# Spreading a softmax's inverse sums over 64 rows by transfers through device memory instead of by TensorE, ScalarE and VectorE

## What is computed

```python
h = relu(layernorm(x))
q2, k2, v2 = heads(h, ...)                    # two projections each; (16, 384, 64)
scores = einsum('hnd,hmd->hnm', q2, k2) / 8 + mask     # mask from 6144 edges
attn = softmax(scores, axis=-1)
out = einsum('hnm,hmd->hnd', attn, v2)
x = x + out.reshape(384, 1024) @ wo.T + bo
# second layer: relational graph convolution; for each of 8 edge types r:
#   mean_r = (counts_r @ h) / max(count, 1);  u += mean_r @ weight[r]
# third: two SAGE layers; fourth: x @ W.T with a sparse W
```

## Time and profile before

| | us |
|---|---|
| runs of the kernel before | 989.72, 989.1 and one outlier of 1886.29; median 989.72 |
| the profiled execution, device time | 988.7 |
| its span in the trace | 986.9 |
| PE busy in the span | 934.6 (95%) |
| DVE, ACT, POOL busy | 614.1, 368.8, 461.9 |

### The profile page before, as it was taken

One profiled execution on the slowest core, in us unless ns is written; L12 is line 12 of the kernel. 1 busy time (PEld: TensorE's weight loads), 2 busy tenths in 40 slices (PEclk: granted clock), 3 DMA queues, 4 the chain that ended last, 5 costly groups with the idle time before them and its releaser, 6 DMA issues.

```text
span 986.9 us, 13646 instructions
## 1 busy us (share of the span) xinstructions
PE 934.6 (95%) x4743; PEld 823.6 (83%) x4743; DVE 614.1 (62%) x1001; ACT 368.8 (37%) x583; POOL 461.9 (47%) x413
## 2 busy tenths in 40 slices
PE   4999999998999789999999999999999959999994
PEld 4999999997889778888888888888888848878883
DVE  6998888867883525655656556565657366445535
ACT  6333333346883343222222322232243234244311
POOL 5324435455564450756547475474759003216212
PEclk8999999999999989999999999999999979999997
DMA  8998766542345364443453544543333603232301
GB/s 204 243 262 232 207 161 160 144 105 17 50 72 170 65 193 145 115 142 107 143 160 106 162 106 141 150 120 97 97 107 128 212 26 136 99 107 99 115 22 64
DMA packets 89796, 128.09 MB, mean 130 GB/s; under 512 B 34488, under 2 KB 67472, under 8 KB 89744
## 3 DMA queue, kind: packets, MB, share of 16 engines
q1 hardware_dynamic: 72640, 123.02, 41.8%
q0 software_dynamic: 15584, 0.11, 3.9%
q10 hardware_dynamic: 1520, 4.30, 1.2%
HBM read 116.65 MB, written 7.59 MB: 126 GB/s over the span
## 4 chain that ended last, share of the span: by engine, by line
PE 85%; DMA 6%; DVE 3%; POOL 3%; issue 2%; ACT 1%; SPq 0%; POOLq 0%; DVEq 0%; ACTq 0%
PE ps L609 48%; PE ps L437 20%; PE ps L656 8%; DMA count_d<-met,cell 4%; PE ps L554 2%; PE ps L527 2%; POOL count_d L1543 1%; PE ps L490 1%; PE ps L414 1%; DMA raw<-in_L_gnn_root 1%; DMA b_in<-in_L_gnn_bo 1%; DVE stats L1070 1%; PE ps L760 1%; PE ps L644 1%; DVE h L1422 0%
## 5 line engine op out<-in xcount | busy, mean ns | idle before, releaser
L1195 DVE TENSOR_TENSOR wlo<-raw,whi 128x1024 fp32r<-128x1024 f32 x120 | 204.3, 1705 | 141.9 <-ACT whi L845 141.8
L437 PE MATMUL ps<-acts,whi 128*128 128x384 f32 (+1 forms) x896 | 230.3, 338 | 0.0
L1573 POOL TENSOR_TENSOR mean_lo<-mean_f,mean_hi 128x384 fp32r<-128x384 f32 x80 | 92.4, 1155 | 196.2 <-ACT mean_hi L989 196.2
L437 PEld LDWEIGHTS ps<-acts,whi 128*128 128x128 f32 x896 | 161.8, 189 | 0.9 <-issue 0.5
L989 ACT ACTIVATE mean_hi<-mean_f 128x384 fp32r<-128x384 f32 x80 | 42.0, 525 | 299.0 <-DVE mean_f L1331 299.0
L437 PE MATMUL ps<-acts,wlo 128*128 128x384 f32 (+1 forms) x448 | 150.4, 336 | 0.0
L609 PE MATMUL ps<-whi,mean_hi 128*128 128x512 f32 x480 | 149.4, 392 | 0.0
L609 PE MATMUL ps<-whi,mean_lo 128*128 128x512 f32 x480 | 148.8, 391 | 0.0
L609 PE MATMUL ps<-wlo,mean_hi 128*128 128x512 f32 x480 | 148.6, 391 | 0.0
L845 ACT ACTIVATE whi<-raw 128x1024 fp32r<-128x1024 f32 x120 | 125.4, 1048 | 27.1 <-PE ps L609 21.7
L1594 POOL DMA_INDIRECT weight_d<-weight_sum,cell x48 | 95.8, 1996 | 30.7 <-DMA weight_d<-weight_sum,cell 19.3
(11 more groups left out here) (177 smaller groups left out, 1419.4 us busy)
## 6 DMA issues: line engine op xcount, KB each, us to landing
raw<-in_L_gnn_weight SPq DMA_DIRECT2D x64, 512.0 KB
rows_b<-rows_d SPq DMA_DIRECT2D x24, 384.0 KB, 5.2
raw<-in_L_gnn_w_gate SPq DMA_DIRECT2D x16, 512.0 KB
raw<-in_L_gnn_W_self SPq DMA_DIRECT2D x16, 512.0 KB
raw<-in_L_gnn_W_neigh SPq DMA_DIRECT2D x16, 512.0 KB
count_d<-total_r SPq DMA_DIRECT2D x8, 576.0 KB
rel_r<-count_d SPq DMA_DIRECT2D x8, 576.0 KB, 4.5
raw<-in_L_gnn_wq SPq DMA_DIRECT2D x32, 128.0 KB
```

The costliest lines, as they stand in the source:

```text
L437: mm = pe.matmul(ps[:, j % 2, 0:N], stationary[j % RING][:, k, :], acts[:, a, moving, k, :], start=i == 0, stop=i == 3 * KT - 1)
L1195: dve.tensor_tensor(wlo_row[slot], raw[slot][:, :], whi_row[slot].bitcast(F32), ALU.subtract)\
L1573: pool.tensor_tensor(mean[1][:, k % 2, :], mean_f[:, k % 2, :], mean[0][:, k % 2, :].bitcast(F32), ALU.subtract).then_inc(S["mean_lo"], 1)
```

## The change

Per pair, SP writes the 768 inverses of both heads (`rinv`, 128 partitions x 6) to device memory, `inverse_d`, each to its node's place. It waits for that to land, and reads each head's row of 384 back, repeated over 64 partitions, straight into `o_f`. The copy on DVE, the three turns on PE and the copy on ACT are gone, and with them `rinv_cols`. The three transfers stand in SP's program between the stages of the pair's even and odd head. `rinv` is single, so DVE's reciprocals of the next pair wait for the write of the pair before; `make_pair` now waits for the two reads.

```diff
-            rinv_cols = sb("rinv_cols", [P, 2, NT, P], F32, scope)
...
+        inverse_d = nc.dram_tensor("inverse_d", (H // 2, 2, N), F32, kind="Internal").ap()
...
-            for o in range(H):
-                stage_v(o)
+            def spread(pair):
+
+                sp_.wait_ge(S["sum_inverted"], 2 * pair + 2)
+                sp_.dma_start(inverse_d[pair].rearrange("e (t p) -> p e t", p=P), rinv[:, :, :],
+                               allow_slow_non_contiguous=True)\
+                   .then_inc(S["inverse_out"], 16)
+                sp_.wait_ge(S["inverse_out"], 16 * (pair + 1))
+                for e in range(2):
+                    sp_.dma_start(o_f[DH * e:DH * e + DH, pair, :], inverse_d[pair, e].partition_broadcast(DH))\
+                       .then_inc(S["spread_in"], 16)
+
+            for pair in range(H // 2):
+                stage_v(2 * pair)
+                spread(pair)
+                stage_v(2 * pair + 1)
...
-            def spread_sums(pair):
-
-                pe.wait_ge(S["sum_inverted"], 2 * pair + 2)
-                if pair:
-                    pe.wait_ge(S["spread_read"], pair)
-                else:
-                    pe.wait_ge(S["v_lo"], KT)
-                for nt in range(NT):
-                    mm = pe.transpose(ps[:, 7, P * nt:P * nt + P], rinv_cols[:, pair % 2, nt, :], ident[:, :])
-                mm.then_inc(S["spread_made"], 1)
...
-                spread_sums(pair)
...
-            def read_spread(pair):
-                act.wait_ge(S["spread_made"], pair + 1)
-                act.activation(o_f[:, pair, :], ps[:, 7, 0:N], ACT.Copy).then_inc(S["spread_read"], 1)
...
-                read_spread(pair)
...
             def invert_sums(o):
-                d0 = DH * (o % 2)
                 dve.wait_ge(S["exp_ready"], 6 * (o // 2) + 5 + o % 2)
-                link(dve.reciprocal(rinv[:, o % 2, :], rsum[:, o % 4, :]))
-                dve.tensor_copy(rinv_cols[:, o // 2 % 2, :, d0:d0 + DH],
-                                rinv[:, o % 2, :].unsqueeze(2).to_broadcast([P, NT, DH])).then_inc(S["sum_inverted"], 1)
+                need(dve, S["inverse_out"], 16 * (o // 2))
+                dve.reciprocal(rinv[:, o % 2, :], rsum[:, o % 4, :]).then_inc(S["sum_inverted"], 1)
...
             def make_pair(pair):
-                dve.wait_ge(S["spread_read"], pair + 1)
+                dve.wait_ge(S["spread_in"], 16 * 2 * (pair + 1))
                 dve.wait_ge(S["pv_done"], 2 * pair + 2)
```

More of the change, by code:

```diff
@@ L121, in build @@
             pt = [sb(f"pt_{s}", [P, 2, NT, N], F32R, scope) for s in ("hi", "lo")]
-            rinv_cols = sb("rinv_cols", [P, 2, NT, P], F32, scope)
-            sb("rest_of_place_3", [P, 2 * KT * N - 4 * NT * N - 2 * NT * P], F32, scope)
+            sb("rest_of_place_3", [P, 2 * KT * N - 4 * NT * N], F32, scope)
             v_st = sb("v_st", [P, 2, 2, NT, P], F32R, scope)
@@ L176, in build @@
             v_cleared v_made v_turned v_hi v_lo
-            scores_ready scores_read exp_ready sum_inverted
-            probs_turned pt_hi pt_lo pv_done spread_made spread_read pair_made pair_hi pair_lo last_lo
+            scores_ready scores_read exp_ready sum_inverted inverse_out
+            probs_turned pt_hi pt_lo pv_done spread_in pair_made pair_hi pair_lo last_lo
             y_evacuated y_turned y_added
```

## The result

| | before | after |
|---|---|---|
| runs, us | 989.72, 989.1, 989.25 and the outlier | 1039.06, 1036.03, 1035.4, 1034.82 |
| median, us | 989.49 | 1035.72 |
| the profiled execution, us | 988.7 | 1039.06 |
| its span, us | 986.9 | 1037.2 |
| PE busy, us | 934.6 | 947.1 |

The account below looks back on a forecast made before the run. ACT following PE's full attention bodies was taken to set POOL's `pair_low` of pair 5, then counts. Savings of 0.64 + 0.4 + 1.3 + 0.4 = 2.7 us gave 986.0, 987.0 as the runs' median; range 984.5 to 991.5.

Parts of the forecast that it names:

- What bounds the kernel: PE, then ACT up to POOL's `pair_low` of pair 5, then counts until `root` tiles; PE idles 2.67 us there.
- Bodies 1 to 6, 0.22 us each: Attention on PE: three turns removed save 0.33 us a body, 0.11 to 0.15 handed back waiting for `pt_lo`; 1.3 in all.
- 2.7 us up to `pair_low` of pair 5: Gain until POOL's last such step: 0.64 + 0.4 in body 0, 1.3 in bodies 1 to 6, 0.4 for ACT's copy.
- The write of the inverses: SP's added write: 768 pieces at 49 ns on 16 engines, 2.4 us of data, landing at 252.7, hidden.
- the prediction's own formula: Write's landing: data 1.25 us after issue, a wait for busy engines, pieces times ns over 16 engines, then 0.4 us.
- the 174: Price in ns a piece of the write at which late stages make the kernel 2% slower, 4.5 us a body.
- The odd stage comes too late: Rival, chance 0.13: SP waits for the write, stalling PE in `weigh_values` above 80 ns a piece; 996.6 us at 120 ns.
- nothing queues at DVE's reciprocals: DVE's reciprocals at 256.11 need the write landed, forecast for 252.7, so no wait there.
- The saving is lost among the transfers: Rival, chance 0.22: added transfers delay POOL's counts or transfer 31; gain -0.5 to 1 us, 989 to 990.2 us.
- Behind the last `pair_low` everything moves as a block: Count transfers, tables and tiles shift together; count transfer 31 might shrink the gain some 2 us or grow it; none taken.
- SP at the last pair: After attention SP reaches the `wo` loads up to 1 us later, which is not on the chain.
- The signs named in the text: Failure if idle before the `root` tile vanishes, POOL waits for DMA before pair 5, or the write exceeds 4 us.

Follow-up runs that it names:

- the kernel with the line moved: Kernel before, with SP loading the last four `root` tiles ahead of its wait for the counts instead of behind it: 983.65 us, ratio 0.9964.
- the turned version: Changed kernel, inverses turned by DVE into 128-byte pieces, odd stage issued ahead of the landing wait: 987.08 us; with the `root` load also moved, 983.71 us.
- The unread write: Kernel before, complete, plus the 4-byte write of the inverses between a pair's stages, which nobody reads: 1006.99 us, ratio 1.0188.

## Why the prediction was wrong, step by step

- **What bounds the kernel** was read rightly for the counts, but one cost was missed: the 2.67 us of idling bring a stretch of half the granted clock, and cost 1.6 us more in all. The 4 us of the kernel with the line moved (interval 2 to 5) agree with both together.
- **Bodies 1 to 6, 0.22 us each**: 0.11. The wait for `pt_lo` was named, but the hand-back was taken at the low end. The removed turns took 0.33 on the chain; PE's busy time fell by 0.24, and idling rose from 0.09 to 0.22.
- **2.7 us up to `pair_low` of pair 5**: 1.8 without the write (290.84 to 289.06). Six bodies of 0.11 are 0.66; that leaves 1.1 for the first body and ACT's copy, where 0.64 + 0.4 + 0.4 = 1.4 had been put.
- **The write of the inverses: this step failed.** It was priced at 49 ns a piece, the dearest row of small pieces at hand, with 20 and 49 as bounds, and so at 4.4 us. It measured 9.1 to 11.8. By the prediction's own formula that is (10.9 - 1.25 - 0.4) x 16 / 768 = 193 ns a piece (184 if the 0.4 us that it let the write wait for busy engines is taken off too), above the 174 from which it had said the kernel loses over 2%. The arithmetic behind it held: (193 - 80) x 48 = 5.4 us a body, 43 us for eight, on 987.0 gives 1030 of the measured 1036. The rows used were of a stage into SBUF and of counts at scattered addresses, and neither has neighbours in device memory. They were no bound for this write.
- **The shape of the price.** Counted per piece it is wrong at any value: 384 pieces take 9.3 us and 768 take 11.1 when 4 bytes apart, 2.7 when 512 apart (medians). The estimate that the prediction took from the Trainium skill (DMA: Bandwidth & Descriptors, Anatomy of one DMA), 2.0 us and nothing for pieces, stands there for transfers that GpSimd issues. It is off by a factor of five for this write of SP's, and near for the same pieces 64 or 512 bytes apart (2.8 and 2.7 us): the measurement decides.
- **"The odd stage comes too late"** was the rival that came true, at 0.13. Its mechanism stood as written: SP waits in order, and PE stalls in `weigh_values`. It left out that the loop closes: once late, SP writes again right behind the stages, the period is landing + 1.2 for the reads (once 3.4) + 1.4 for two stages, and all eight pairs pay, not five. Nor does it hold that nothing queues at DVE's reciprocals: `rinv` is single, and DVE idles 11.4 us ahead of them for the landing, in six waits. PE's long waits all end with a stage, so this second path cost nothing that shows here.
- **"The saving is lost among the transfers"**, at 0.22, assumed bursts of 1 to 2.4 us. The unread write shows that contention is real and worth 19 us with 4-byte neighbours. With pieces of 128 bytes nothing measurable is left of it.
- **"Behind the last `pair_low` everything moves as a block"** does not hold: 1.13 us earlier there and 0.1 later at the end of the counts in the turned version, but 1.78 earlier and 1.5 earlier without the write. These are single executions; that the meeting of counts, tiles and reload decides whether a gain arrives is my reading of them, not shown.
- **SP at the last pair.** The prediction let SP reach the `wo` loads 1 us later "not on the chain". The last stage stands there as well, and 2 us of delay put it behind x's reload: 7 to 8 us of PE's time in two kernels.
- **The signs named in the text** worked: it said that the forecast fails if the write takes over 4 us, and that an idle before the odd head's product, released by a DMA, shows the late stage. Both rows stand above. The two other signs of failure came as well: the idle before the `root` tile is gone, and POOL comes to `pair_low` of pair 5 at 328.98 without waiting for ACT, behind 9.99 us of waiting for a count transfer.

The Trainium skill (DMA: Bandwidth & Descriptors, Specifications) says that below 512 bytes a DMA engine does a read-modify-write. Size alone is not what costs here: pieces of 4 bytes that lie 64 or 512 bytes apart land in 2.7 to 2.8 us. Read-modify-writes of one stretch of memory that must follow one another would fit the table, but no run here shows them, and they would not by themselves say why 16 neighbours cost over four times what 8 do (8.1 against 1.9 us). That stays open. The Trainium skill (DMA: Bandwidth & Descriptors, Terms, and Queues, rings and completion order) says that a strong ordered write, which is what counts a transfer as landed, lands only after every earlier write of that DMA engine. With the odd stage issued right behind the write, a stage that flows in about 1 us landed after 8.2 to 10.5 us, which agrees. It does not say why stages issued ahead of the write landed after 8.1 and 11.7 us as well, so it is at most part of the contention; no run took write and stage apart on different DMA engines.

## What to carry to other kernels

Before writing scalars from many partitions to device memory, ask how close the pieces lie to each other, not only how many and how large they are; where no row of the trace has small neighbours in device memory, the trace gives the price no upper bound. Turn the data on the chip until a piece is 128 bytes, and put nothing urgent behind the wait for its landing, since an engine that issues in order turns a late landing into a loop. And look first at what waits for the work that you save: here one moved line gave 4 us, and the saved work, with its replacement paid, nothing that could be measured.

The best version measured that computes everything is the kernel before with the moved line, 983.65 us; it beats both kernels, and the turned version equals it.

## What the chip showed that I had not expected

The packets of the write are all on record within a microsecond, and the landing comes seven later. In the kernel after, from the issue at 244.51 on (window, us, PE clock, share of the DMA engines' time, GB/s; overlapping packets can take the share over 1), then the queues between 246.3 and 247.2:

```profile
246.25:246.75 0.50, 0.50 1.09 149
246.75:247.25 0.50, 0.50 3.23 3
...
247.75:248.25 0.50, 0.50 0.00 0
```
```profile
q0 software_dynamic: 16, 0.00, 159.3%
q1 hardware_dynamic: 1029, 0.06, 72.9%
...
count_d<-met,cell POOLq DMA_INDIRECT x1, 12.1
```

1029 packets of the stage and the write pass in 0.9 us. From 247.75 to 248.25 nothing is moved, from there to 254.5 only packets of the counts, and SP is released at 254.56. The 16 packets of the counts that start in the same 0.9 us take 1.6 times the whole window of all 16 engines' time, and the count transfer issued there lands after 12.1 us. So a view of packets and bytes would have priced this write at under a microsecond; only its landing tells.
